# Narrow back transposes, 1/std spread by matmuls, and earlier loads at three stage borders of a ConvNeXt block with a fixed-point convolution behind it

## The chip, the cores and the metric

The kernel runs on one core of a Trainium2 chip. The metric is the device time of one execution in microseconds; the median of three runs of the kernel before is 1080.56 us (1080.2 to 1081.1).

## What is computed

```python
# x: (16, 96, 56, 56) fp32
y = depthwise_conv7x7(x, dw_w) + dw_b
y = transpose(y, (0, 2, 3, 1))                       # channels last
y = (y - mean_c(y)) * rsqrt(var_c(y) + 1e-6) * ln_w + ln_b
h = gelu(y @ w1 + b1)                                # 96 -> 384
gx = sqrt(sum over h,w of h*h)                       # per image and hidden channel
nx = gx / (mean_hidden(gx) + 1e-6)
h = grn_gamma * (h * nx) + grn_beta + h
z = x + transpose(h @ w2 + b2)
w = power_of_two(clamp(weight)); zq = floor(z * 65536) / 65536, clipped
out = depthwise_conv3x3(zq, w) + floor_to_fixed(bias)
```

## The kernel before, in words

Three stages run one after the other, with DRAM between them (`y_scratch`, `z_scratch`). All waits are semaphores written by hand; each engine runs its own instruction list in order.

**Stage a** is the 7x7 convolution. It goes over 24 batches of 4 channels (CB), and a batch has 4 groups s. `load_rows` (L321) brings 16 images of 4 channels into `xin`. `tin` (L552) turns them on TensorE, ACT's `xt_copy` (L691) and DVE's `low_part` (L894) split the result into a high and a low fp32r part. Each channel is then convolved by 12 matmuls (`convolve`, L573) with banded weight tables. The tables come from the 49 taps: DVE writes them into `la` (L832), SP stores `la` to DRAM as `lines_a` (L341 to L343) and reads it back shifted, one diagonal per partition (`load_tables`, L354); ACT rounds them (`table_high`, L722), POOL makes the remainder (`table_low`, L471). ACT evicts each channel with its bias (`yt_copy`, L706). `back` (L600) turns each group of the previous batch back with 8 transposes of 64 pixels x 112 rows, alternating between partitions 64 to 127 and 0 to 63; ACT's `out_copy` (L716) reads 56 of each 64 columns, reversed, into `ost`, and SP stores the batch (L371). In its loop SP loads batch b+1 and stores batch b-3. Beside this DVE and POOL keep a running mean and a running sum of squares over the 96 channels (`update`, L919, L921, L923, and POOL's L486), with pixels on the partitions and 448 columns: 28 pairs of rows of 16 images.

**Between a and the MLP** one chain makes 1/std for all 448 columns: variance on DVE (L929), square root on ACT (L765), reciprocal and a Newton step (L942 to L946), reordering (`in_order`, L938), 8 transposes (L634), a copy (L950), a store to DRAM (`stats_scratch`, L767) and loads that broadcast each image's row to 96 partitions (`rb`, L771 to L773). SP loads `y` of image 0 (L401) after all stores of y have landed.

**The MLP** goes over 16 images of 7 tiles of 448 pixels. `scale` (L964, y times 1/std), `high` (L969) and POOL's `low` (L497) feed `up` (L643 to L645, 9 matmuls of a tile), ACT applies gelu (L787) and sums squares (`squares`, L755). `step(i)` runs `up` of image i beside `down` (L653, 3 fp32 matmuls of a tile) of image i-1, because the global response norm needs the sums of a whole image: `grn_sums` (L977), POOL's square root (L506), a matmul with ones (L667), `grn_scale` (L983 to L994). Hence in `step(0)` TensorE has no `down` to run. DVE rounds and SP stores z (`store_z`, L417); ACT's `with_constant` (L762) scales x for the residual.

**Stage c** is the 3x3 convolution, built like a with 4 matmuls for a channel, its own tables (L523 on POOL) and evictions shared by ACT and DVE (L1079, L1068). It starts when the last z has landed: SP loads batch 0 of z, DVE clears the halos of `xt` (L812). SP loads the tables of batch b in turn b, and stores batch b-3.

## Time and profile before

| | |
|---|---|
| median of 3 runs | 1080.56 us |
| the profiled execution, its own time | 1080.37 us |
| span of the profile | 1078.6 us |
| TensorE busy | 990.8 us (92%) |
| VectorE, ScalarE busy | 825.5 us, 830.8 us (77% each) |
| GpSimd busy | 411.7 us (38%) |
| mean granted clock of TensorE | 0.963 |

The profile is one execution. Its page gives busy shares in 40 slices, and the trace behind it gives each instruction with its start, its length and what released it. Engines: PE is TensorE, PEld its weight loads, DVE VectorE, ACT ScalarE, POOL GpSimd, SP SyncE; a q behind the name means the queue that issues a DMA. "us from start" counts from the first instruction. A merged row "x8" begins with the first of eight instructions and lasts until the end of the last.

### The profile page before, as it was taken

The numbers are of one execution on the slowest core, as the hardware profiler recorded it, in microseconds if no ns is written. First come the engines' busy times: TensorE is split into PE (matmuls) and PEld (weight loads), VectorE is DVE, ScalarE is ACT, GpSimd is POOL, SyncE is SP. The second block draws the span as 40 slices with busy tenths as digits, with TensorE's granted clock in tenths as the row PEclk, the third lists the DMA queues.
The fourth block names the chain that finished last, engine by engine and source line by source line (L and its number), as shares of the span: only waits on it lengthen the run. The fifth ranks groups of instructions, "written<-read, shape, count | busy, mean of one in ns | idle before, by whom it ended". The sixth has DMA issues, their size and how long they took to land.

```text
span 1078.6 us, 21092 instructions
## 1 busy us (share of the span) xinstructions
PE 990.8 (92%) x5574; PEld 717.7 (67%) x5574; DVE 825.5 (77%) x1768; ACT 830.8 (77%) x1724; POOL 411.7 (38%) x353
## 2 busy tenths in 40 slices
PE   3999999999999467999999999999999849999996
PEld 2788888888888355666666666666666427767774
DVE  7777777777777565888888888888887667888885
ACT  2688888888887357898988888888888607787874
POOL 2666676666666153332333333333332001111110
PEclk9999999999999766999999999999999978999999
DMA  8777777777772592555555555555543247999995
GB/s 162 147 183 182 181 179 184 187 187 179 180 179 66 131 225 82 157 175 163 172 162 171 172 162 170 162 171 162 167 136 90 80 110 187 245 248 243 247 244 154
DMA packets 146312, 182.95 MB, mean 170 GB/s; under 512 B 13799, under 2 KB 140424, under 8 KB 143208
## 3 DMA queue, kind: packets, MB, share of 16 engines
q1 hardware_dynamic: 145480, 179.97, 62.5%
q10 hardware_dynamic: 800, 2.61, 1.0%
q8 instruction: 13, 0.21, 0.1%
q14 instruction: 19, 0.16, 0.0%
HBM read 124.28 MB, written 58.25 MB: 169 GB/s over the span
## 4 chain that ended last, share of the span: by engine, by line
PE 71%; DVE 12%; ACT 6%; issue 6%; DMA 3%; DVEq 1%; POOL 0%; ACTq 0%; SPq 0%; POOLq 0%
PE psum L573 22%; PE psum L653 21%; PE psum L643 6%; PE psum L644 6%; PE psum L645 6%; PE psum L552 6%; PE psum L600 3%; DVE arena_r L894 3%; ACT arena L706 2%; ACT arena_r L691 2%; DVE arena L919 1%; DMA arena<-lines_a 1%; DVE arena L923 1%; DVE arena L1079 1%; DVE arena L1068 1%
## 5 line engine op out<-in xcount | busy, mean ns | idle before, releaser
L573 PE MATMUL psum<-arena_r 112*128 112x464 f32 x1536 | 375.2, 386 | 0.3 <-issue 0.2
L573 PEld LDWEIGHTS psum<-arena_r 112*128 112x128 f32 x1536 | 276.8, 190 | 33.9 <-issue 1.1
L653 PE MATMUL psum<-arena,w2s 128*96 128x448 f32 x672 | 266.8, 542 | 2.8 <-DVE w2s L994 2.8
L787 ACT ACTIVATE arena<-psum,b1g 128x448 f32<-128x448 f32 x336 | 201.8, 630 | 58.3 <-PE psum L645 58.2
L497 POOL TENSOR_TENSOR arena_r<-arena,arena_r 96x448 fp32r<-96x448 f32 x112 | 134.1, 1197 | 268.7 <-DVE arena_r L969 194.8
L653 PEld LDWEIGHTS psum<-arena,w2s 128*96 128x96 f32 x672 | 109.8, 164 | 119.1 <-issue 111.8
L643 PE MATMUL psum<-arena_r,w1h 96*128 96x448 f32 x336 | 154.1, 459 | 14.2 <-POOL arena_r L497 13.0
L706 ACT ACTIVATE arena<-psum,bias_a 64x224 f32<-64x224 f32 (+1 forms) x288 | 117.0, 442 | 61.8 <-PE psum L573 50.6
L894 DVE TENSOR_TENSOR arena_r<-psum,arena_r 112x224 fp32r<-112x224 f32 x384 | 127.2, 382 | 48.3 <-ACT arena_r L691 47.5
L691 ACT ACTIVATE arena_r<-psum 112x224 fp32r<-112x224 f32 x384 | 112.6, 355 | 54.8 <-PE psum L552 52.5
L486 POOL TENSOR_TENSOR arena<-arena 128x448 f32<-128x448 f32 x96 | 110.0, 1146 | 109.8 <-DVE arena L923 109.2
L552 PE MATMUL psum<-ident,arena 112*112 112x112 f32 x768 | 109.1, 278 | 43.1 <-DMA arena<-in_x_dram 16.0
L755 ACT ACTIVATE arena<-arena 128x1792 bf16<-128x1792 f32 (+1 forms) x96 | 144.5, 1505 | 2.2
L471 POOL TENSOR_TENSOR arena_r<-arena,arena_r 112x512 fp32r<-112x512 f32 x96 | 123.6, 1300 | 20.5 <-ACT arena_r L722 20.5
L644 PE MATMUL psum<-arena_r,w1h 96*128 96x448 f32 x336 | 126.2, 376 | 0.0
L645 PE MATMUL psum<-arena_r,w1l 96*128 96x448 f32 x336 | 125.9, 375 | 0.0
L552 PEld LDWEIGHTS psum<-ident,arena 112*112 112x112 f32 x768 | 77.9, 139 | 58.0 <-issue 21.9
L919 DVE TENSOR_TENSOR arena<-arena,psum 128x448 f32<-128x448 f32 x96 | 59.6, 621 | 74.3 <-ACT arena L706 74.2
L706 ACT ACTIVATE arena<-psum,bias_c 64x224 f32<-64x224 f32 (+1 forms) x216 | 88.0, 442 | 15.8 <-PE psum L573 13.9
L1002 DVE TENSOR_TENSOR psum<-arena,psum 96x448 f32<-96x448 f32 x112 | 69.6, 621 | 39.5 <-PE psum L653 39.0
L600 PEld LDWEIGHTS psum<-ident,arena 64*112 64x112 f32 x1536 | 57.5, 130 | 62.7 <-issue 57.8
L523 POOL CAST arena_r<-arena 112x1024 fp32r<-112x1024 bf16 x24 | 25.0, 1043 | 180.3 <-DMA arena<-lines_c 153.7
(94 smaller groups left out, 1146.1 us busy)
## 6 DMA issues: line engine op xcount, KB each, us to landing
arena<-lines_a SPq DMA_DIRECT2D x48, 448.0 KB
arena<-in_x_dram SPq DMA_DIRECT2D x48, 392.0 KB
y_scratch<-arena SPq DMA_DIRECT2D x48, 392.0 KB
arena<-in_x_dram SPq DMA_DIRECT2D x112, 168.0 KB, 2.5
z_scratch<-arena SPq DMA_DIRECT2D x112, 168.0 KB, 2.0
arena<-z_scratch SPq DMA_DIRECT2D x48, 392.0 KB
out_dram<-arena SPq DMA_DIRECT2D x48, 392.0 KB
arena_r<-y_scratch SPq DMA_DIRECT2D x98, 168.0 KB, 2.6
```

Source lines behind the costliest of these rows:

```text
L497: pool.tensor_tensor(yl[:, CH * t:CH * t + CH], ct[:, (t + p) % 2, :], yh[:, CH * t:CH * t + CH].bitcast(F32), ALU.subtract).then_inc(yn_r ...
L552: mm = nc.tensor.transpose(p_in[s % 2][0:PAIR, at:at + CM], xin[:, p, IG // 2 * s + i, PAIR * h:PAIR * h + PAIR], ident[0:CM, 0:CM])
L573: mm = nc.tensor.matmul(p_conv[s % 2][:, 0:NCOL], w[:, p, s, TW * k:TW * k + TW], v[:, p, s, slot0 + k:slot0 + k + JP, :].rearrange("p j i ...
L643: nc.tensor.matmul(p_h[m][:, 0:CH], w1h[:, w], yh[:, cols], start=True, stop=False)
L644: nc.tensor.matmul(p_h[m][:, 0:CH], w1h[:, w], yl[:, cols], start=False, stop=False)
L645: nc.tensor.matmul(p_h[m][:, 0:CH], w1l[:, w], yh[:, cols], start=False, stop=True).then_inc(h_done, 1)
L653: mm = nc.tensor.matmul(p_o[k][0:C, 0:CH], w2s[:, p, m, :], hid[:, p, m, CH * t:CH * t + CH], start=(m == 0), stop=(m == MT - 1))
L691: ins = nc.scalar.activation(tile_group(xt_h, p, s, h), bank_group(s, h), ACT.Identity)
L706: ins = nc.scalar.activation(to[part, q], cols[part, :, :, j:j + 2 * NRUN - 1:2], ACT.Identity, bias=bias[part, bass.ds(n, 1)], scale=scale)
L755: nc.scalar.activation(sqd[:, 0:CH * (t1 - t0)], hid[:, p, m, CH * t0:CH * t1], ACT.Square, accum_out=ss[:, p, m, part:part + 1]).then_inc ...
L787: nc.scalar.activation(hid[:, p, m, CH * t:CH * t + CH], p_h[m][:, 0:CH], ACT.Gelu, bias=b1g[:, m:m + 1]).then_inc(gelu_done, 1)
L894: ins = dve.tensor_tensor(tile_group(xt_l, p, s, h), bank_group(s, h), tile_group(xt_h, p, s, h).bitcast(F32), ALU.subtract)
```

## The change

It has eight parts.

1. **Back transposes** (stages a and c) take 56 pixels, not 64; the tables are read with another offset so that the 56 results lie at columns 0 to 55. `forwards` follows.
2. **Start.** The eleven small loads go from SP's queue to ACT's; ACT issues them first, and waits for them only before its first `yt_copy`. DVE clears the halos, then writes `la` with one strided copy in place of 49. The first four tables are loaded each by its own pair of DMAs (`t_first`). `convolve` waits for each channel's table alone. ACT runs one square root at the start.
3. **Stores** run at b-2 in place of b-3, in both stages; in c the tables are loaded one batch ahead.
4. **Last batch of a.** Its four backs use two pairs of PSUM banks in turn. The last update leaves out the mean.
5. **The chain for 1/std** runs first for the 56 columns of images 0 and 1 (EARLY), between ACT's `out_copy` of groups 0 and 1 of the last batch; the other 392 follow in pieces between DVE's tiles of image 0 (`other_images`).
6. **Spread.** For images 0 and 1, 1/std reaches the 96 partitions through TensorE: for each tile 8 fp32 matmuls, with one column of `rstd` broadcast as a weight of 56 x 96 and the reversed identity `rev` (56 x 56) as the moving side. `scale` reads the result in PSUM. Two tiles come before `up(0, 0)`, one behind each `up(0, t)`, five behind `step(0)`. The rows for the other images are turned (4 transposes), copied and stored to DRAM after image 1's `scale` and `high`; ACT waits for that store before the gelu of image 1.
7. **y of image 0** goes to a place of its own (`y0`): channels 0 to 87 from DRAM once 22 batches are stored, the last 8 channels straight from `ost`, in 8 DMAs of one channel each. SP's order around it is new.
8. **Border to c.** z of images 0 to 13 and the first tables are loaded before the last image's `down`; POOL clears the halos; TensorE doesn't wait for the last residual; only images 14 and 15 (one pair of columns) are loaded after the last store of z.

```diff
@@ offsets and narrow back
-    return bass.AP(tensor=v.tensor, offset=v.offset + LSTEP - 1,
-                   ap=[part, [LSTEP, n], [bank, 2], [-1, W]])
+    return bass.AP(tensor=v.tensor, offset=v.offset + W - 1,
+                   ap=[part, [W, n], [bank, 2], [-1, W]])
...
-                            mm = nc.tensor.transpose(outs[s % len(outs)][0:CM, 1 - r, LSTEP * n:LSTEP * n + LSTEP],
-                                                     yt[q:q + LSTEP, p, i, (h + 1 - r) % 2].rearrange("p g m -> p (g m)"),
-                                                     ident[q:q + LSTEP, q:q + LSTEP])
+                            mm = nc.tensor.transpose(outs[s % len(outs)][0:CM, 1 - r, W * n:W * n + W],
+                                                     yt[q:q + W, p, i, (h + 1 - r) % 2].rearrange("p g m -> p (g m)"),
+                                                     ident[q:q + W, q:q + W])
@@ SP, start and stage a
+            for k in range(CB):
+                for r in range(2):
+                    shifted = bass.AP(tensor=lines_a, offset=k * (KA * TW) + LPAD + r * LSTEP - (W - 1), ap=[[1, W], [1, KA * TW]])
+                    sp.dma_start(toep[W * r:W * r + W, 0, k, :], shifted).then_inc(t_first[k], 16)
...
-                        if not (isinstance(b, int) and b < 3):
-                            store(b - 3, 1 - s)
+                            tables(b + 1, 1 - s)
+                        if not (isinstance(b, int) and b < 2):
+                            store(b - 2, s)
...
+            def first_y(b):
+
+                sp.wait_ge(stages["a"]["out"], G * b + 1)
+                for k in range(CB):
+                    c = CB * b + k
+                    sp.dma_start(y0[c:c + 1, :].rearrange("o (m t) -> o m t", t=RUN),
+                                 ost[CR // CB * k:CR // CB * (k + 1), b % 2, 0, :]).then_inc(y0_in, 16)
+
+            sp.wait_ge(stages["a"]["st0"], 32 * (LATE // 2 + LATE % 2))
+            sp.wait_ge(stages["a"]["st1"], 32 * (LATE // 2))
+            sp.dma_start(y0[0:CB * LATE, :], y_v[0][0:CB * LATE]).then_inc(y0_in, 16)
+            for b in range(LATE, NBATCH):
+                first_y(b)
+                store_y(b, b % 2)
...
-            load_y(0, 0)
-            sp.wait_ge(r_in[0], 16)
-            load_y(1, 1)
+            sp.dma_start(yraw[:, 1, :], y_v[1]).then_inc(y1_in, 16)
             for t in range(NCH):
                 load_x(0, t)
+            sp.wait_ge(stat_rows, 1)
+            sp.dma_start(st_dram.ap().rearrange("(g i) (m t) -> (i m) g t", i=IG, t=PAIR),
+                         res1.rearrange("p (g t) -> p g t", g=G)).then_inc(stat_out, 16)
+            sp.wait_ge(stat_out, 16)
@@ SP, border to c
+            sp.wait_ge(o_done, NCH * (NIMG - 1))
+            for k in range(4):
+                sp.wait_ge(z_out[k], 16 * Z_USES[k % 2] * (NIMG // 2 - 1))
+            first_rows(0, NI2 - 1, c_early)
+            tables_c(0, 0)
             step(NIMG, 0, more_y=False, more_x=False)
             for k in range(4):
                 sp.wait_ge(z_out[k], 16 * Z_USES[k % 2] * NIMG // 2)
-            load_rows(stages["c"], z_v, 0, 0)
-            sp.wait_ge(halo, 2)
+            first_rows(NI2 - 1, NI2, stages["c"]["x0"])
@@ TensorE
+            def spread(i, t):
+
+                n = NCH * i + t
+                to = p_spread[n % 2]
+                if n == 1:
+                    pe.wait_ge(stages["a"]["out"], C)
+                need(pe, scale_done, n - 1)
+                for k in range(4):
+                    m, h = 2 * t + k // 2, k % 2
+                    for half in range(2):
+                        at = 2 * NRUN * ((h + half) % 2) + NRUN * i + m
+                        rows = slice(LSTEP * half, LSTEP * half + W)
+                        mm = nc.tensor.matmul(to[:, half, W * k:W * k + W], rstd[rows, at:at + 1].to_broadcast([W, C]), rev[rows, :],
+                                              start=True, stop=True)
+                mm.then_inc(spread_done, 1)
...
                     if t < NCH and not tail:
                         up(i, p, t)
+                    if head and t < NCH:
+                        spread(*divmod(t + 2, NCH))
...
+                if head:
+                    for t in range(2, NCH):
+                        spread(1, t)
+                    stat_rows_out()
@@ ScalarE
+            act.wait_ge(prep, 3)
+            nc.scalar.activation(gnx[:, :], halves[:, :], ACT.Sqrt)
...
-                        out_copy(NBATCH - 1, s, 1)
+                        if s == 1:
+                            act.wait_ge(var_ready, 1)
+                            nc.scalar.activation(root[:, 0:EARLY], var[:, 0:EARLY], ACT.Sqrt).then_inc(root_ready, 1)
+                        out_copy(NBATCH - 1, s, 1, p_last)
...
                 need(act, o_done, NCH * (i - 1))
+                if fixed and i == 1:
+                    act.wait_ge(stat_out, 16)
@@ VectorE
-            for dy in range(7):
-                for dx in range(7):
-                    at = (dy + 1) * LSTEP + dx - 3
-                    ins = dve.tensor_copy(la[:, at:at + 1], wa[:, 7 * dy + dx:7 * dy + dx + 1])
-            link(ins)
...
                 if head:
                     for t in range(1, NCH):
                         normalise(0, 0, t)
+                        other_images(t - 1)
                     for t in range(NCH):
-                        if t == NCH - 1:
-                            grn_sums(i, p)
                         normalise(1, 1, t)
+                    statistics_out()
+                    grn_sums(i, p)
                     return
```

## Rows read from the trace of the kernel before

**Rows 1.** The page, part 2: busy tenths and granted clock in 40 slices.
```profile
PE   3999999999999467999999999999999849999996
PEclk9999999999999766999999999999999978999999
```

**Rows 2.** Sums by stretch: us, busy (x) by engine, clock, DMA share, GB/s.
```profile
30.00:330.00 300.00, 296.91 (x2043) 243.29 (x2042) 224.98 (x436) 240.95 (x595) 205.03 (x171) 0.99 0.71 177
900.00:1078.00 178.00, 162.48 (x1478) 120.29 (x1476) 140.60 (x341) 134.09 (x380) 22.94 (x22) 0.99 0.86 229
```

**Rows 3.** Timeline of the start: us from start, length, engine, line, [idle before].
```profile
5.51 3.05 DVE L832 COPY arena<-arena 96x1 f32<-96x1 f32 x49
...
11.25 0.76 SPq L354 DMA_DIRECT2D arena<-lines_a  x2
...
23.67 3.76 PE L573 MATMUL psum<-arena_r 112*128 112x464 f32 x12
...
26.59 0.63 ACT L722 ACTIVATE arena_r<-arena 112x512 fp32r<-112x512 f32 x1 [2.92 <-DMA arena<-lines_a]
```

**Rows 4.** Timeline of TensorE, end of stage a; the last row is a later back.
```profile
346.05 0.44 PE L600 MATMUL psum<-ident,arena 64*112 64x64 f32 x8
346.42 2.79 PE L573 MATMUL psum<-arena_r 112*128 112x464 f32 x12
...
363.67 0.64 PE L600 MATMUL psum<-ident,arena 64*112 64x64 f32 x8 [0.64 <-ACT arena L716]
```

**Rows 5.** Timeline in stage c: TensorE waiting once in a batch.
```profile
1057.14 0.59 PE L552 MATMUL psum<-ident,arena 112*112 112x112 f32 x4 [0.35 <-DVE arena_r L894]
```

**Rows 6.** Timeline between stage a and the first up.
```profile
359.77 0.62 DVE L919 TENSOR_TENSOR arena<-arena,psum 128x448 f32<-128x448 f32 x1 [1.15 <-ACT arena L706]
...
374.66 0.40 ACTq L767 DMA_DIRECT2D stats_scratch<-arena  x1
...
379.21 0.34 ACTq L771 DMA_DIRECT2D arena_r<-stats_scratch  x1
...
382.92 0.62 DVE L964 TENSOR_TENSOR arena<-arena_r 96x448 f32<-96x448 f32 x1 [8.29 <-DMA arena_r<-stats_scratch]
...
385.29 0.74 PE L643 MATMUL psum<-arena_r,w1h 96*128 96x448 f32 x1 [11.32 <-POOL arena_r L497]
```

**Rows 7.** Sums by stretch, columns as in rows 2: the last stored batch.
```profile
349.00:353.00 4.00, 4.00 (x32) 3.15 (x31) 2.26 (x4) 2.44 (x6) 1.63 (x2) 1.00 0.72 192
353.00:357.00 4.00, 4.00 (x26) 3.30 (x25) 2.21 (x4) 2.65 (x7) 1.84 (x2) 1.00 0.00 0
```

**Rows 8.** Timeline: small matmuls with weight loads (96 columns, fp32).
```profile
36.95 0.59 PE L539 MATMUL psum<-bet,w2r 128*96 128x1 f32 x6
```

**Rows 9.** Timeline of the head of the MLP.
```profile
391.46 0.61 DVE L964 TENSOR_TENSOR arena<-arena_r 96x448 f32<-96x448 f32 x1
...
393.25 0.61 DVE L964 TENSOR_TENSOR arena<-arena_r 96x448 f32<-96x448 f32 x1
...
414.34 0.59 PE L667 MATMUL psum<-gx,ones 128*128 128x3 f32 x2 [4.92 <-POOL gx L506]
...
421.65 2.48 PE L653 MATMUL psum<-arena,w2s 128*96 128x448 f32 x6
```

**Rows 10.** Sums by stretch, columns as in rows 2: the granted clock in the head.
```profile
390.00:394.50 4.50, 4.50 (x13) 3.98 (x13) 4.40 (x6) 1.95 (x4) 3.85 (x3) 0.50 0.99 231
394.50:400.00 5.50, 5.50 (x28) 4.98 (x28) 5.13 (x7) 5.43 (x9) 3.86 (x4) 1.00 1.02 257
416.00:421.80 5.80, 5.80 (x17) 5.05 (x17) 2.08 (x6) 3.65 (x6) 1.45 (x1) 0.50 0.00 0
```

**Rows 11.** Timeline of the border to stage c.
```profile
878.87 1.84 SPq L321 DMA_DIRECT2D arena<-z_scratch  x4
...
885.29 1.72 PE L552 MATMUL psum<-ident,arena 112*112 112x112 f32 x8 [12.70 <-DMA arena<-z_scratch]
...
891.63 1.90 PE L573 MATMUL psum<-arena_r 112*128 112x464 f32 x4
```

More of the change, by code:

```diff
@@ L198, in build @@
         sqd = mlp(128, SQ_WIDE // 2).bitcast(BF16)
+        hid = [hid0, mlp(128, MT, HW)]
+        y0 = hid[1][0:C, MT - 1, :]
+        ct = mlp(C, 2, CH)
+        rstd, var, root, rstd_in, newton, res1 = [conv(TW, NPIX) for _ in range(6)]
+        res1 = res1[0:IG * NPAIR, :]
+        assert conv.at <= mlp.at - 2 * CH - HW
         BANK = 512
@@ L215, in build @@
         dw_in = sem("dw_in")
+        t_first = [sem(f"t_first{k}") for k in range(CB)]
         consts = sem("consts")
@@ L362, in tables_c, with conv_transfers @@
                 load_tables(stages["c"], lines_c, KC, toep_b, b, s)
-            def conv_transfers(S, src, dst, tables, ahead):
+            def conv_transfers(S, src, dst, tables):
                 runs_of = dst.rearrange("(i g) c (m t) -> g (c m) i t", g=2, t=RUN)
@@ L485, in add @@
                     need(pool, m2_done, n)
-                    pool.tensor_tensor(m2, m2, dsq[:, k % 2, :], ALU.add).then_inc(m2_done, 1)
+                    cols = slice(EARLY, NPIX) if last and k == 2 * CB - 1 else slice(0, NPIX)
+                    pool.tensor_tensor(m2[:, cols], m2[:, cols], dsq[:, k % 2, cols], ALU.add).then_inc(m2_done, 1)
             bodies(pool, add)
@@ L512, in _ @@
             steps(pool, step)
+            pool.wait_ge(h_done, MT * NCH * NIMG)
+            for v in (xt_h, xt_l):
+                for slots in (slice(0, HALO), slice(HALO + NPAIR, SLOTS)):
+                    pool.memset(v[:, :, :, slots, :].bitcast(F32), 0.0).then_inc(halo, 1)
             S = stages["c"]
@@ L545, in tin @@
                     n = G * b + s
-                    if s == 0:
+                    if S is stages["c"] and isinstance(b, int) and b == 0:
+                        if s == 0:
+                            pe.wait_ge(c_early, 32)
+                        if s == G - 1:
+                            pe.wait_ge(S["x0"], 32)
+                    elif s == 0:
                         pe.wait_ge(S[f"x{p}"], 16 * (b - p) + 32)
@@ L636, in _ @@
-            mm.then_inc(stat_t, 1)
+                    if S is stages["c"]:
+                        back_waits(NBATCH - 1, s)
+                        back(NBATCH - 1, s, 1)
+                    else:
+                        if s == 0:
+                            evicted(pe, S, NBATCH - 1, CB - 1)
+                        pe.wait_ge(S["out"], G * (NBATCH - 1) + max(s - 1, 0))
+                        back(NBATCH - 1, s, 1, p_last)
+            conv_stage(stages["a"], KA, 0, ((toep_h, xt_h), (toep_h, xt_l), (toep_l, xt_h)), bias_products)
@@ L950, in _, with other_images @@
-            dve.tensor_copy(res1.rearrange("p (g h w) -> p g h w", g=G, h=2), forwards(p_stat[0:IG * NPAIR], G)).then_inc(stat_rows, 1)
+            inverse(early)
+            refine_square(early)
+            refine(early).then_inc(first_ready, 1)
+            dve.wait_ge(m2_done, C)
+            dve.tensor_scalar(var[:, EARLY:NPIX], m2[:, EARLY:NPIX], 1.0 / C, LN_EPS, ALU.mult, ALU.add).then_inc(var_ready, 1)
+            def other_images(k):
+                middle = (EARLY + NPIX) // 2
+                if k == 0:
+                    dve.wait_ge(root_ready, 2)
+                    inverse(slice(EARLY, middle))
+                elif k == 1:
+                    inverse(slice(middle, NPIX))
+                elif k == 2:
+                    refine_square(slice(EARLY, NPIX))
+                elif k == 3:
+                    link(refine(slice(EARLY, NPIX)))
+                elif k == 4:
+                    in_order(rstd_in, rstd).then_inc(stat_in, 1)
```

217 lines of the change are left out of this document (115 added, 102 removed).

## The prediction

> **What bounds the kernel now.** I read the page's slices first, then sums by stretch, then the timeline at each border. The slices [rows 1] show TensorE at nine tenths nearly everywhere, with three holes: the first slice, the fourteenth and fifteenth (stage a to MLP) and the thirty-third and its neighbours (MLP to stage c). The granted clock falls only at the last two. Inside stage a TensorE is busy 296.91 of 300 us, inside stage c 162.48 of 178 with the DMA rate at 229 GB/s [rows 2]. So two kinds of time can be won: TensorE's own work in a and c, and the length of the holes. In steady MLP nothing is changed. The sum is made against the profiled execution, 1080.37 us (span 1078.6, 1.8 around it), which is 0.2 below the median of 1080.56; I don't correct for that.
>
> **Start.** DVE spends 3.05 us on 49 one-column copies; the tables' first loads are issued at 11.25; the first convolution starts at 23.67; ACT then waits until 26.59 for the tables of batch 1 and sits ahead of the eviction that TensorE needs [rows 3]. The order of the bytes is the point: x of batch 0, small loads, `la`, tables 0, x 1, tables 1. `la` is ready some 5 us earlier (3.05 for the copies, the rest because halo, mean and m2 memsets now stand elsewhere), but its store lies behind the 0.8 MB of x in SP's queue, and the small loads, now on ACT's queue, share the DMA engines with that x. What goes away is the idle time between the end of those loads and the tables, about 1.5 to 2.5 us. Bounds: 0.8 (all hidden behind x) and 3.05 (the whole copy row). Eight table loads in place of two cost six more issues (0.38 each, half of the 0.76 row), in which x 1 is issued later, but the queue is full then. I take **2.0**.
>
> **Narrow back.** Eight transposes last 0.44 and the next convolution starts 0.37 after them; at half clock the eight last 0.64 [rows 4]. The extra 0.20 for one halving of the clock, over four pairs (the two halves of the partitions run side by side), is about 0.05 a pair, that is 64 columns at two clocks each at 2.4 GHz (53 ns). With 56 columns a pair takes 47 ns: 4 x 6.7 = 27 ns less for a group. In stage a TensorE never waits, so 96 groups give **2.6**. Ends: 0 if the weight load sets the pace (its 112 columns stay), 0.37 x 8/64 = 46 ns x 96 = 4.4 if the whole row shrinks. The granted clock fits the moving side, so I stay at 27 ns.
>
> The Trainium skill, "TensorE: Matmul & The Clock Gate", section "LDWEIGHTS (loading the stationary operand)", says that a weight load takes time by its columns, and that the rows don't matter. By it, 112 columns at 1.2 GHz would be 93 ns a load, as before the change, and the narrow back would bring nothing. The pair step of about 53 ns [rows 4] lies below that figure, so the trace speaks against it as the bound here; it is a rival below because only the load's width is unchanged.
>
> In stage c TensorE waits 0.35 us in a batch for DVE's `low_part` [rows 5]. Two of the four backs of a batch lie on the stretch between DVE's release and that wait, so what they save is waited for; the other two count: 2 x 27 ns x 24 = 1.3, up to 2.6 with all four, 0 if DMA binds (229 GB/s). I take 1.6. Stores one batch earlier and tables one batch ahead move SP's issues: SP now stops about one channel for `out`, but its next load is a batch away, so 0. Stage c: **1.6**.
>
> **Border a to MLP.** Before, DVE's last `dev` starts at 359.77, the stats store is issued at 374.66 and lands at 379.21 (4.55), the broadcasts let the first `scale` start at 382.92, and the first `up` starts 2.37 later, at 385.29 [rows 6]. After:
> - The early chain has 56 columns and leaves out the mean, a table load and the transposes. I estimate 363; it is not what comes last.
> - y0: batch 21's store is over by 353, as the DMA is empty from 353 to 357 at a rate of 192 before [rows 7]. 88 channels are 1.10 MB, at 192 GB/s 5.7 us plus some 2, so 361. Batch 22's store (0.8 MB, 4.2 us) stands ahead of the last four one-channel loads in the same queue: 360.3 + 1 + 4.2 + a little = 366.3. This comes last. First `scale` 366.3 (16.6 earlier), first `up` 368.7.
> - Then TensorE has more work: 14 spreads of 8 fp32 matmuls, 16 instructions each with its load. Six small ones with 96 weight columns take 0.59 [rows 8]; less about 0.2 for the last one's own length, over five steps, that is some 80 ns apart. 16 x 80 = 1.3 alone; if the halves overlap, half of it, 0.65; 1.6 with a turn at each end. I take 1.3, and 2.4 at half clock. At 1.2 GHz an `up` takes 9 x 0.373 = 3.36, at 2.4 GHz 1.86: 13 matmuls in 4.50 and 28 in 5.50 [rows 10]. The clock returned at 394.5, 9.2 after the first `up`. So two tiles at half clock, 2 x (3.36 + 2.4) = 11.5, and five at 1.86 + 1.3 = 15.8, with 0.5 for ACT's squares: the last of nine spreads ends at about 396.5.
> - Image 1's tiles follow at the pace of DVE and POOL, 1.79 (391.46 to 393.25) [rows 9], five after the first: its last `scale` is over at 406, `high` 406.6, the copy 407.2 (0.6, a DVE copy of 448 columns as the tile row), the store of the rows 4.55 on [rows 6]: 411.8.
> - A new wait: ACT may not start the gelu of image 1 before that. Queued behind it on ACT are `with_constant` and all gelus, and TensorE's `up(1, 1)` waits for the banks. So 411.8 + 1.3 = 413.1, then two `up` at half clock, 6.7, or 5.0 at ACT's pace: the first `down` at 418.1 to 419.8. Before it was 421.65 [rows 9]. SP waits for the same store with `load_next(2)` and `store_z` behind it; DVE needs image 2 only with the first `down`, 3 us later, so 0.
> Of 16.6 us won at the head's start only **3.0** are left. The `grn_sums` chain (414.34 before) is ready by about 409 and no longer decides.
>
> **Border to c.** Before, z of batch 0 and 1 (1.6 MB) is issued at 878.87, the first turn of x starts at 885.29, the first convolution at 891.63, since `tin` of batch 1 stands ahead of it [rows 11]. After, 0.70 MB of that is there already and POOL clears the halos (DVE's part was hidden behind z's landing). 0.70 MB at 170 to 190 GB/s is 3.7 to 4.1. Of this some 0.8 goes back: more matmuls of the first batch run before the clock returns. **3.2**, between 1.5 and 5.5. The extra issues on SP (4, 1.8 us) fall between the last load of x and the first store of image 15, where SP waits for DVE anyway. If that were full, the store would be late by as much, but z's ring has four slots.
>
> **Sum.** 2.0 + 2.6 + 3.0 + 3.2 + 1.6 = 12.4. 1080.37 - 12.4 = **1068.0**.
>
> **Rivals.**
> - *A quick head*: halves of the spreads overlap (0.65) and the clock is back two tiles earlier. Nine spreads then end about 5 us earlier and the two `up` run at full clock. The border gives 9: 1062.0. For it: pairs overlap in the back [rows 4]. Chance 0.2.
> - *A slow head*: spreads 1.6, clock up a tile later, DVE's tiles longer with the pieces of `other_images` between (5.6 us in all). 4 us back: the border gives -1 to 0, the start 1: 1072.5. Chance 0.2.
> - *The weight load sets the back's pace*: no 2.6, no 1.6: 1072.2. Chance 0.05.
> - *Slower*: the spreads are small matmuls between loads; if the clock stays at 1.2 GHz through the whole head, seven tiles take 7 x (3.36 + 2.7) = 42.4 from 368.7, five spreads 13.5 more, to 424.6, then 7.6 for turning, copy, store and ACT, and 6.7 for two `up`: the first `down` at 438.9, 17.3 later than before. With 9.4 won elsewhere the time is 1088.3. It decides as soon as the head loses more than 9.4. Against it: continuous `up` brought the clock back before [rows 10]. Chance 0.03. That 56 rows would break the overlap of the two halves (0.16 for a group, 31 us over both stages) belongs to the same side: 0.02.
> - *The change doesn't do what it says*: y0 lands late, as some wait on SP stands ahead; then the head starts later, up to 3 us: 1071. It counts with the slow head.
> The forecast itself has 0.5.
>
> **How the numbers follow.** Range 1060.5 to 1075: from a quick head with 1.5 more at the start and in c, down to a slow head with both c terms at their low end. About 0.8 of the chance lies in it. A measurement can tell some 0.2% (2 us) from no change. Faster 0.93, same 0.02, slower 0.05.
>
> **What would show it.** Back rows of 0.41 in place of 0.44 and a period of a channel at the end of a of 3.06 in place of 3.09; tables' first loads issued near 9.7; the first `scale` near 366.3 behind a y load; spreads of about 1.3 at 2.4 GHz; ACT's wait ahead of image 1's gelu on the stats store; first `down` near 418.7; first convolution of c about 4 us after the last store of z less than before. It is wrong if y0 isn't the last to come, if the clock is at 1.2 GHz during image 0 for more than 12 us, or if the period of stage a doesn't shrink.

## The result: 58 us slower

The changed kernel takes 1138.55 us (median of 4 runs, 1138.03 to 1140.16) against 1080.58: a ratio of 1.0539, interval 1.052 to 1.0557. The forecast was 1068.0. The profiled execution has a span of 1138.3 against 1078.6, so 59.7 us have to be found.

The page's slices, as in [rows 1], with the DMA row of both kernels (the last line is the DMA row of the kernel before). A slice is 28.5 us here, 27.0 before:

```profile
PE   2999999999998999999999999999997768768766
PEclk9999999999998559999999999999999798987888
DMA  7377677777764325555555555555324676675674
...
DMA  8777777777772592555555555555543247999995
```

The hole between stage a and the MLP (14th and 15th slice before) is nearly filled, but the clock there is lower. From the 31st slice on, TensorE is at six to eight tenths where stage c had it at nine. DMA is not full there either, at four to seven tenths where it was at nine. The sums by stretch, as in [rows 2], say the same: stage a is as before, and in stage c TensorE is busy 139.17 of 178 us in place of 162.48, at 172 GB/s in place of 229.

```profile
30.00:330.00 300.00, 296.11 (x2044) 243.61 (x2044) 221.07 (x434) 241.37 (x595) 204.98 (x171) 0.99 0.69 173
900.00:1078.00 178.00, 139.17 (x1122) 104.63 (x1123) 108.79 (x264) 106.21 (x301) 18.06 (x18) 0.88 0.67 172
```

From the start times of TensorE's matmuls in both traces (first and last convolution of a stage, first and last `down`) the 59.7 us split as follows (changes in us, less is faster):

| stretch | before | after | forecast | measured |
|---|---|---|---|---|
| start, to the first convolution | 23.67 | 24.80 | -2.0 | +1.1 |
| stage a, first to last convolution | 334.43 | 333.96 | -2.6 | -0.5 |
| last convolution of a to first `down` | 63.55 | 67.65 | -3.0 | +4.1 |
| first to last `down` | 450.40 | 450.26 | 0 | -0.1 |
| last `down` to first convolution of c | 19.58 | 15.78 | -3.2 | -3.8 |
| stage c, first to last convolution | 175.80 | 234.58 | -1.6 | +58.8 |
| last convolution to the end | 11.17 | 11.27 | 0 | +0.1 |

Each column is one trace. Other kernels below run the same code in some of these stretches, and their traces show the spread: with the changed start the first convolution comes at 23.8 to 25.1, the changed stage a takes 334.0 to 334.9, and the stretch up to the first `down` 66.2 to 67.7. The kernel before and before_c_store2, alike up to stage c, differ there by 0.3, 0.6 and 1.2. A difference under about 1 us between two traces is therefore not shown.

**Stage c.** The timeline of SP's queue and of TensorE's `tin` (us from start, length, engine, line, [idle before <- what ended it]). The changed kernel: SP's rows, then the `tin` with which TensorE begins three successive batches.

```profile
948.87 0.90 SPq L366 DMA_DIRECT2D out_dram<-arena  x2
950.05 3.36 SPq L329 DMA_DIRECT2D arena<-z_scratch  x2
953.61 0.98 SPq L349 DMA_DIRECT2D arena<-lines_c  x2
956.33 0.90 SPq L366 DMA_DIRECT2D out_dram<-arena  x2
957.78 3.18 SPq L329 DMA_DIRECT2D arena<-z_scratch  x2
961.16 0.93 SPq L349 DMA_DIRECT2D arena<-lines_c  x2
969.44 0.90 SPq L366 DMA_DIRECT2D out_dram<-arena  x2
970.62 3.34 SPq L329 DMA_DIRECT2D arena<-z_scratch  x2
...
958.97 1.74 PE L585 MATMUL psum<-ident,arena 112*112 112x112 f32 x8 [4.54 <-DMA arena<-z_scratch]
...
967.46 0.98 PE L585 MATMUL psum<-ident,arena 112*112 112x112 f32 x8
...
979.52 1.74 PE L585 MATMUL psum<-ident,arena 112*112 112x112 f32 x8 [4.54 <-DMA arena<-z_scratch]
```

Every load of z (L329) is issued 1.2 to 1.5 us behind a store (L366), never on its own. Two batches take 979.52 - 958.97 = 20.55 us, 10.3 for one in place of 7.46 before. The loop can be read off: `tin` 958.97, then 10.5 us until the output is ready and the store goes out at 969.44, the load behind it at 970.62, and 8.9 us until that load lets the next `tin` start. The sum of what SP waited for (900 to 1100 in the changed kernel; us in total, times, longest):

```profile
SPq L366 <- DVE arena L1181: 89.2, 19, 10.0
SPq L329 <- PE psum L585: 0.5, 1, 0.5
```

The same of before, 900 to 1078:

```profile
SPq L371 <- DVE arena L1068: 45.4, 24, 6.5
SPq L321 <- PE psum L552: 39.1, 20, 4.6
```

Before, SP arrived early at the load and waited there for TensorE to leave the buffer (39.1 us in 20 waits). Now it waits only at the store: it always comes too late to the load.

In stage a (60 to 340) the waits moved in the same way, first the changed kernel, then before:

```profile
SPq L366 <- ACT arena L796: 157.8, 20, 8.3
SPq L329 <- PE psum L585: 3.5, 2, 2.0
...
SPq L321 <- PE psum L552: 93.1, 19, 5.3
```

There the later loads cost nothing: a batch of stage a lasts 13.9 us, and TensorE waits for x only 0.4 us in all.

### The profile page after: what moved, and what is told of

Its sections match the earlier page's. It is cut to its first block, busy times and chain, and to the rows that moved or that the text cites. A ratio compares the mean times of both kernels' runs of the same rounds, so it can differ in the third digit from the quotient of the medians.

```text
span 1138.3 us, 21578 instructions
## 1 busy us (share of the span) xinstructions
PE 1033.3 (91%) x5794; PEld 755.6 (66%) x5794; DVE 816.8 (72%) x1715; ACT 832.6 (73%) x1725; POOL 410.0 (36%) x360
## 4 chain that ended last, share of the span: by engine, by line
PE 68%; DMA 10%; DVE 9%; ACT 5%; issue 4%; SPq 3%; DVEq 0%; ACTq 0%; POOL 0%; POOLq 0%
PE psum L710 20%; PE psum L606 20%; DMA arena<-z_scratch 7%; PE psum L700 7%; PE psum L701 6%; PE psum L702 6%; PE psum L585 5%; ACT arena L786 3%; PE psum L633 2%; DMA arena<-in_x_dram 2%; SPq L329 2%; DVE arena_r L967 2%; PE psum L683 1%; DVE arena L1181 1%; DVE arena L998 1%
## 5 line engine op out<-in xcount | busy, mean ns | idle before, releaser
L606 PE MATMUL psum<-arena_r 112*128 112x464 f32 x1536 | 384.4, 393 | 0.3 <-issue 0.2
L606 PEld LDWEIGHTS psum<-arena_r 112*128 112x128 f32 x1536 | 283.6, 195 | 32.3 <-issue 1.0
L520 POOL TENSOR_TENSOR arena_r<-arena,arena_r 96x448 fp32r<-96x448 f32 x112 | 131.1, 1170 | 279.3 <-DVE arena_r L1085 202.4
L585 PE MATMUL psum<-ident,arena 112*112 112x112 f32 x768 | 117.0, 292 | 83.7 <-DMA arena<-z_scratch 51.8
L700 PE MATMUL psum<-arena_r,w1h 96*128 96x448 f32 x336 | 157.6, 469 | 4.9 <-POOL arena_r L520 3.2
L585 PEld LDWEIGHTS psum<-ident,arena 112*112 112x112 f32 x768 | 84.0, 147 | 97.5 <-issue 57.1
L493 POOL TENSOR_TENSOR arena_r<-arena,arena_r 112x512 fp32r<-112x512 f32 x96 | 123.7, 1301 | 20.4 <-ACT arena_r L804 20.4
L701 PE MATMUL psum<-arena_r,w1h 96*128 96x448 f32 x336 | 129.0, 384 | 0.0
L702 PE MATMUL psum<-arena_r,w1l 96*128 96x448 f32 x336 | 128.6, 383 | 0.0
L633 PEld LDWEIGHTS psum<-ident,arena 56*112 56x112 f32 x1536 | 58.8, 135 | 66.0 <-issue 61.9
```

The lines of the kernel that those rows point to most:

```text
L493: pool.tensor_tensor(toep_l[:, p, s, :], toep[:, p, s, :], toep_h[:, p, s, :].bitcast(F32), ALU.subtract).then_inc(A["tl"], 1)
L520: pool.tensor_tensor(yl[:, CH * t:CH * t + CH], ct[:, (t + p) % 2, :], yh[:, CH * t:CH * t + CH].bitcast(F32), ALU.subtract).then_inc(yn_r ...
L585: mm = nc.tensor.transpose(p_in[s % 2][0:PAIR, at:at + CM], xin[:, p, IG // 2 * s + i, PAIR * h:PAIR * h + PAIR], ident[0:CM, 0:CM])
L606: mm = nc.tensor.matmul(p_conv[s % 2][:, 0:NCOL], w[:, p, s, TW * k:TW * k + TW], v[:, p, s, slot0 + k:slot0 + k + JP, :].rearrange("p j i ...
L700: nc.tensor.matmul(p_h[m][:, 0:CH], w1h[:, w], yh[:, cols], start=True, stop=False)
L701: nc.tensor.matmul(p_h[m][:, 0:CH], w1h[:, w], yl[:, cols], start=False, stop=False)
```

## Experiments on the slow stage c

**c_store3**, the changed kernel with stores of c at b-3:

```diff
-                        if not (isinstance(b, int) and b < 2):
-                            store(b - 2, s)
+                        if not (isinstance(b, int) and b < lag):
+                            store(b - lag, (s + lag) % 2)
```

`lag` is 3 in stage c and 2 in stage a.

> Edit: the changed kernel, but in stage c batch b-3 is stored in body b, as before the change, where the changed kernel stores batch b-2 (tables stay one batch ahead, stage a stays as changed). Theory (the store of b-2 waits for an output that TensorE finishes only a batch later, and the load behind it on SP's queue starts too late): stage c falls back to its old length, 187 us from its first convolution at about 892.5, so 1080 to 1082 us, ratio to the changed kernel 0.949 to 0.951; SP's wait at the store no longer stands just ahead of each load, and TensorE's wait for the z load (44.8 us) goes. Rival (tables moved one batch ahead, or the narrow back, lengthen stage c): stays near 1138.

Measured: 1079.6 us, ratio to before 0.9997 (0.9987 to 1.0007). Stage c takes 175.10 us. SP waits at the load again:

```profile
SPq L366 <- DVE arena L1181: 50.8, 24, 6.6
SPq L329 <- PE psum L585: 40.3, 20, 5.0
```

The one line is worth 59 us, and the rest of the change is worth nothing in sum.

**c_tables_behind**, tables of c in turn b again, stores left at b-2:

```diff
-                            tables(b + 1, 1 - s)
+                            if ahead:
+                                tables(b + 1, 1 - s)
+                        if not ahead and not (isinstance(b, int) and b == 0):
+                            tables(b, s)
```

> Edit: the changed kernel, but in stage c the tables of batch b are loaded in body b, as before the change; the stores stay at b-2. Theory (store order): nothing is won, 1135 to 1141 us. Rival (two table loads between x and the store make the queue late): near 1081 us.

Measured: 1160.72 us (one run). Both were wrong: it is 22 us slower still. The tables of the batch now stand behind the late load too. So the tables one batch ahead, which I had no price for, soften the loss.

**before_c_store2**, the kernel before with only c's stores moved to b-2:

```diff
-                        if not (isinstance(b, int) and b < 3):
-                            store(b - 3, 1 - s)
+                        if not (isinstance(b, int) and b < lag):
+                            store(b - lag, (s + lag) % 2)
```

`lag` is 2 in stage c and 3 in stage a.

> Edit: the kernel before the change, with one thing changed: in stage c batch b-2 is stored in body b. Theory (store order alone makes the loss): stage c takes 10.2 to 10.3 us for a batch in place of 7.46, so 1080.6 + 22 x 2.8 = 1136 to 1142 us. Rival (the loss needs the tables ahead or the narrow back as well): below 1100 us.

Measured: 1159.78 us (one run), 79 more than before and 18 above the theory's range. The store order alone makes the loss; the theory had taken its size from the changed kernel, whose tables are ahead. c_tables_behind, 0.9 away, is the same case.

**c_pool_store**, the same lag of two, but stores of c issued by POOL, behind its copy of the tables:

```diff
+                    if not (isinstance(b, int) and b < 2):
+                        store(b - 2, p)
...
+            def store(b, s):
+                pool.wait_ge(S["out"], G * b + G)
+                for g in range(2):
+                    pool.dma_start(out_of[g][bass.ds(b * CR, CR)], ost[CR * g:CR * g + CR, s, :, :]).then_inc(S[f"st{s}"], 16)
```

> Edit: the changed kernel (stores of batch b-2 in body b), but in stage c the stores are issued by POOL, behind its copy of the tables of batch b, so that no load stands behind them. Theory (only the order on SP's queue makes the loss: a load waits behind a store whose output isn't ready): 1078 to 1084 us. Rival (storing b-2 rather than b-3 is bad in itself, since store and load then fall together on the DMA engines): 1130 us or more.

Measured: 1081.91 us (one run). Bytes, buffers and lag are those of the changed kernel; only the load no longer stands behind the store and its wait for `out`. In c_store3 the stores do stand ahead of the loads on SP's queue, but of a batch that is ready sooner, and nothing is lost. The two together settle it: it is a load behind a wait on one queue, not the traffic. DMA is back at 241 GB/s between 900 and 1050 (c_store3: 240, the changed kernel: 175).

## Experiments on the other terms

**before_narrow**, the kernel before with the narrow back alone (the first part of the change, with the copy of the turned statistics adapted).

> Edit: the kernel before the change, with the narrow back alone (56 columns a transpose in place of 64, both stages). Theory of the prediction (moving columns set the pace): 2.6 us less in stage a and 1.6 in c, 1076.4 us, ratio 0.9961. Rival (the weight load, whose 112 columns stay, sets the pace): 0 to 0.8 us less, 1079.8 to 1080.6; the period of a batch in stage a of the changed kernel, 13.88 against 13.90, speaks for this one.

Measured: 1079.21 us, ratio 0.9994 (0.9985 to 1.0003). Stage a takes 334.07 us in place of 334.43, stage c 175.08 in place of 175.80. A back is 0.42 or 0.43 us in place of 0.44 [rows 4]:

```profile
345.26 0.42 PE L600 MATMUL psum<-ident,arena 56*112 56x56 f32 x8
345.61 2.80 PE L573 MATMUL psum<-arena_r 112*128 112x464 f32 x12
348.34 0.43 PE L600 MATMUL psum<-ident,arena 56*112 56x56 f32 x8
```

The rival of the weight load is nearer in its number. An eighth of the moving columns is gone, and the stages are 0.36 and 0.72 us shorter where 2.6 and 1.6 were forecast; the first of these is within the spread of one trace. The start times of the transposes are firmer: from the first of a group of eight to the last it is 216 ns before and 206 to 208 with the narrow back, so 8 to 10 ns of the 27 forecast for a group, or 0.7 to 0.9 us for the 96 groups of a stage (an estimate from these times). At 2.4 GHz two successive pairs start 56 ns apart with 64 columns and 54 to 55 with 56. At 1.2 GHz they start 107 ns apart with 64 columns (before) and 93 to 95 with 56 (the changed kernel): there the step did shrink by an eighth.

**c_border_late**, c_store3 with `first_rows` and the tables loaded only behind the last store of z (two blocks of SP's list exchanged).

> Edit: c_store3 without the early load at the border to c: the rows of batch 0 of images 0 to 13 and the tables are loaded only behind the last store of z, as before the change. Theory (the early 0.70 MB give the 3.8 us by which stage c starts sooner): the first convolution of c comes 3.5 to 4.2 us later than in c_store3, 1083 to 1084 us. Rival (POOL's clearing of the halos in place of DVE's gives it): no difference, 1079.6 us.

Measured: 1082.83 us, 3.2 more than c_store3; from the last `down` to c's first convolution 19.03 us in place of 15.50. The early load gives the border's gain, as forecast.

**head_warm**, c_store3 with TensorE kept busy before the first `up`:

```diff
+            def warm(times):
+                for _ in range(times):
+                    nc.tensor.matmul(bank[2][:, 0:HID], w1h[:, 0:128], w1h[:, :], start=True, stop=True)
...
                         back(NBATCH - 1, s, 1, p_last)
+                        warm((9, 1, 5, 3)[s])
...
+            warm(26)
             steps(pe, step)
```

> Edit: c_store3 with TensorE kept busy in the pauses between stage a and the first up: 44 matmuls of 384 columns whose results nobody reads (9, 1, 5 and 3 behind the four last backs of stage a, 26 behind the second spread). Theory (the pauses between 359.5 and 370.9 bring the clock to 0.5, and the spreads between the ups keep it there till 426): the granted clock stays at 1.0, a tile of image 0 takes 1.86 + 0.8 = 2.7 us in place of 5.12, then DVE, POOL and the stats store set the pace; first down at 404 to 410 in place of 426.4, so 1079.6 less 16 to 22: 1058 to 1064 us. Rival (spreads of 56 columns lower the clock by themselves): the clock falls to 0.5 some tiles in, less than 8 us won, above 1071 us.

Measured: 1072.04 us, ratio to before 0.9917 (0.99 to 0.9935). A gain of 7.6 us over c_store3, where the theory had 16 to 22; the number is the rival's, its mechanism is not, since the spreads between the `up` ran at 1.00. The granted clock fell all the same before them, behind the pause of 1.6 us that lies ahead of the first of these matmuls. At 1.2 GHz they took too long: the first `up` came at 378.21 in place of 370.61. By then the clock was up again, and a tile of image 0 took 2.82 us. At the end of the head ACT still waited 4.56 us for the store of the statistics' rows.

**head_light**, each spread replaced by two wide matmuls; it leaves out 1/std of images 0 and 1, so only its time is of use:

```diff
-                for k in range(4):
...
-                        mm = nc.tensor.matmul(to[:, half, W * k:W * k + W], rstd[rows, at:at + 1].to_broadcast([W, C]), rev[rows, :],
-                                              start=True, stop=True)
+                for half in range(2):
+                    mm = nc.tensor.matmul(to[:, half, :], w1h[:, 0:C], w1h[:, 0:4 * W], start=True, stop=True)
```

> Edit: c_store3 with each spread's eight fp32 matmuls of 56 columns replaced by two single-pass matmuls of 224 columns that write other numbers (1/std of images 0 and 1 is left out). Nothing keeps the clock up in the pauses. Theory (the many small matmuls between the ups keep the clock down): the clock is back at 1.0 some 9 us after the first up, near 379, as in the kernel before; first down near 402 to 408; 1056 to 1062 us. Rival (the clock stays at 0.5 for another reason, such as the head's waits): only the spreads' own length goes, 14 x 1.1 = 15.4 us at most, of which DVE's pace of 1.8 us a tile takes back some; the clock stays at 0.5 till past 400, and the first down comes at 412 or later: 1065 us or more.

Measured: 1067.1 us (one run). The time and the first `down` (412.49) lie in the rival's range, the clock does not: it came back at about 385, 15 us behind the first `up` and not 9, and fell again ten microseconds later (columns as in [rows 2], the granted clock third from the end):

```profile
384.00:390.00 6.00, 5.46 (x27) 4.78 (x26) 4.20 (x9) 5.24 (x9) 2.03 (x3) 0.91 0.00 0
390.00:396.00 6.00, 3.63 (x20) 2.66 (x18) 4.02 (x8) 6.00 (x10) 3.30 (x4) 0.95 0.00 0
396.00:402.00 6.00, 5.22 (x17) 4.36 (x17) 5.76 (x9) 4.27 (x7) 4.08 (x5) 0.50 0.00 0
```

From 390 to 396 ACT is busy all the time and TensorE 3.63 of 6 us; the clock is low behind that. So the many small matmuls do hold the clock down (with them it is 0.50 until about 417 in c_store3), but even without them it is slow to return, and once it is up, ACT's pace opens pauses and the clock is lost again.

**head_stat**, c_store3 with the statistics' rows turned and copied in the middle of image 1 and not at the end of the head:

```diff
+                    if head and t == NCH - 1:
+                        stat_rows_out()
```

> Edit: c_store3 with the turning of the statistics' rows right behind the spread of image 1's tile 1 on TensorE, and their copy on DVE behind tile 1 of image 1, in place of the end of the head on both. Theory (ACT's gelu of image 1 stands behind the stats store, and this sets the first down): the store is issued at about 408 in place of 415, ACT's wait of 6 us goes, and the first down comes 3 to 5 us sooner than 424.6: 1074.6 to 1076.6. Rival (at the low clock the spreads and ups themselves are the bound, and the wait hides behind them): less than 1 us.

Measured: 1078.74 us, ratio 0.9987 (0.9978 to 0.9997); last convolution of a to first `down` 65.4 us in place of 66.3. The rival: ACT's wait of 6 us is gone and 0.9 us are won, so at the low clock spreads and `up` are the bound and the wait lay mostly beside them.

**start_order**, c_store3 with the convolution of batch 0 ahead of the `tin` of batch 1, in both stages.

> Edit: c_store3 with one change of TensorE's order: in batch 0 of both stages the convolution of a channel stands ahead of the tins of batch 1. Theory (both stages' first convolution waits for x of batch 1, whose tin stands ahead of it, and not for the tables): stage a's first convolution starts near 21 in place of 24.1 (POOL is done with the low tables at 20.3), stage c's near 887 to 889 in place of 892.1; but the matmuls of batch 0 then run until the same x, so 1.5 to 4 us less in all: 1075.5 to 1078. Rival (the tables or the turned x of batch 0 are late too): both first convolutions move by less than 1 us.

Measured: 1079.35 us (one run). The first convolutions moved as the theory said, and stage a's further (16.62 in place of 24.07; 887.07 in place of 891.79), but stage a's last one starts at 358.71 in place of 358.30, and from the last `down` to c's last convolution it is 190.7 us in place of 190.6. An earlier first matmul is worth nothing while the second batch waits for the same load.

**start_x1**, c_store3 with x of batch 1 issued ahead of the tables.

> Edit: c_store3 with x of batch 1 issued in stage a right behind the store of the lines (near 4) and ahead of the tables' first loads, not behind them (13.9). Theory (x of batch 1 is what the start waits for): its landing moves from 22.6 to 15 or 16; the tables land 4 us later than now, at about 20; first convolution at 20 to 22 in place of 24.1; 2 to 4 us less, 1075.6 to 1077.6. Rival (the DMA queue is full until 22 whatever the order, so the tables take the place of x): first convolution at 24 or later, 1079 to 1081.

Measured: 1081.82 us. The first convolution starts at 19.07, better than expected, and the time is 2.2 us worse than c_store3's; stage a's last convolution starts at 361.47 in place of 358.30. What is late next is DVE. Its timeline and POOL's in start_x1:

```profile
17.57 0.16 DVE L922 TENSOR_TENSOR arena<-arena 96x9 f32<-96x9 f32 x1
17.76 1.28 DVE L924 TENSOR_TENSOR arena<-arena 96x9 f32<-96x9 f32 x1
...
21.54 1.20 DVE L928 TENSOR_SCALAR arena<-arena 96x9 uint32<-96x9 uint32 x1
22.77 0.17 DVE L929 TENSOR_TENSOR arena<-arena 96x9 f32<-96x9 f32 x1
...
27.87 1.27 DVE L969 TENSOR_TENSOR arena_r<-psum,arena_r 112x224 fp32r<-112x224 f32 x4
...
17.75 4.96 POOL L495 TENSOR_TENSOR arena_r<-arena,arena_r 112x512 fp32r<-112x512 f32 x4 [15.26 <-ACT arena_r L806]
23.45 2.56 POOL L495 TENSOR_TENSOR arena_r<-arena,arena_r 112x512 fp32r<-112x512 f32 x2 [0.73 <-ACT arena_r L806]
```

The setup of the bias and of c's weights on DVE stands ahead of the low parts of batch 1 and ends only at 27.9. Moving it was not tried.

**all_1**, c_store3 with start_order, start_x1, head_stat, and 36 of the matmuls of head_warm, the first eight of them right behind the last convolution:

```diff
+                        warm((8, 0, 2, 5)[s])
                         if s == 0:
                             evicted(pe, S, NBATCH - 1, CB - 1)
...
+            warm(3)
...
+            warm(18, bank[2])
             steps(pe, step)
```

> Edit: c_store3 with start_order, start_x1 and head_stat together, and with 36 matmuls of 384 columns whose results nobody reads in TensorE's pauses between 359.5 and 370 (8, 2 and 5 ahead of three of the last backs, 3 ahead of the first spread, 18 behind the second), so that the first of them run before the pause that lowered the clock in head_warm. Theory: head near full clock throughout, first up at 370 to 371 in place of head_warm's 378.2, a tile of image 0 2.82 us, first down 404 to 409 in place of 424.6 (15 to 20 less); start 2 to 5 less; border to c 2 to 4 less: 1051 to 1060 us. Rival (the clock falls anyway once the stage a matmuls end, so that the extra matmuls only delay the first up): head wins under 8, 1065 us or more.

Measured: 1058.31 us, ratio 0.9793 (0.9779 to 0.9806). From the last convolution of a to the first `down` 47.0 us, against 66.3 in c_store3 and 63.55 before. The granted clock is 1.00 until 399.

**cold**, all_1 without these 36 matmuls.

> Edit: all_1 without the 36 matmuls in the pauses before the first up; everything else as in all_1. Theory (the clock, kept up by these matmuls, gives the head's 20 us; head_stat alone gave about 1): the clock falls to 0.5 behind the end of stage a and stays there until about 420, a tile of image 0 takes 5.12 us again, the first down comes at 422 to 425 and the time is 1076 to 1079 us. Rival (the three changes of order give it together, since each alone only showed the next wait): below 1066 us.

Measured: 1076.02 us, ratio 0.9963 (0.995 to 0.9976). 17.7 us of all_1's gain hang on matmuls that compute nothing. They do so with head_stat in place: head_warm, without it, won 7.6. The three changes of order give 3.6 us together (c_store3 less cold), where one by one they gave 0.3, -2.2 and 0.9; why they give more together was not taken apart. The sums by stretch (us, busy by PE, PEld, DVE, ACT, POOL, then the granted clock, DMA share, GB/s), first all_1:

```profile
360.00:364.00 4.00, 3.93 (x51) 2.88 (x47) 3.23 (x9) 2.41 (x6) 1.05 (x1) 1.00 0.79 209
364.00:368.00 4.00, 4.00 (x45) 3.94 (x43) 0.74 (x2) 1.60 (x2) 0.00 (x0) 1.00 0.34 94
368.00:376.00 8.00, 6.93 (x57) 5.68 (x57) 5.94 (x8) 3.66 (x6) 3.41 (x3) 1.00 0.74 188
384.00:392.00 8.00, 7.88 (x96) 6.68 (x94) 4.51 (x11) 7.91 (x13) 3.41 (x3) 1.00 0.01 4
```

and cold:

```profile
360.00:364.00 4.00, 1.91 (x28) 1.64 (x28) 2.74 (x9) 2.65 (x7) 1.04 (x1) 0.69 0.82 218
364.00:368.00 4.00, 1.95 (x25) 1.77 (x23) 1.24 (x3) 1.13 (x1) 0.08 (x1) 0.50 0.38 94
368.00:376.00 8.00, 6.90 (x30) 5.79 (x31) 4.12 (x6) 2.16 (x4) 2.66 (x3) 0.50 0.74 191
384.00:392.00 8.00, 8.00 (x40) 6.68 (x39) 4.89 (x8) 2.53 (x4) 2.32 (x2) 0.50 0.01 2
```

The busy shares of 384 to 392 are alike (7.88 and 8.00 of 8), the work done is not: 96 matmuls against 40. A full busy row says nothing of the clock, which stands third from the end.

**warm_c**, all_1 without start_x1, and with 20, 15 and 8 such matmuls behind the `tin` of groups 1, 2 and 3 of c's batch 0.

> Edit: all_1 without start_x1, and with matmuls whose results nobody reads at the border to c as well: 20, 15 and 8 behind the tins of x of batch 0 (groups 1, 2 and 3). Theory: the granted clock stays at 1.0 from 860 to 876 where all_1 had 0.50 to 0.74; the first four channels of c take 1.3 us each in place of 1.9, 1 to 3 us less in c's first batch; the start is 1 to 2 us better or worse, within what start_x1 showed: 1055 to 1058 us. Rival (z of batch 1 landing near 870, not the clock, sets the start of c): c's last convolution moves by less than 0.5 us against its last down, 1058 to 1060 us.

Measured: 1060.07 us, ratio 0.9803 (0.9789 to 0.9816). The clock stays at 1.00 until 872, and yet from the last `down` to c's last convolution it takes 189.4 us in place of 190.1: 0.7 won, next to the rival's limit of 0.5. TensorE then waits for z of batch 1:

```profile
869.14 1.08 PE L611 MATMUL psum<-arena_r 112*128 112x464 f32 x4
872.13 1.25 PE L590 MATMUL psum<-ident,arena 112*112 112x112 f32 x8 [1.91 <-DMA arena<-z_scratch]
```

The rival's mechanism: there a load sets the start, and a faster engine only waits for it. The ratios of warm_c and all_1 overlap, so neither is shown to be the faster. The 1.8 us between their medians are no more than the difference that their traces show from stage a to the first `down` (48.8 and 47.0), where the two kernels do the same.

## Why the prediction was wrong

**Stage c (the step that failed).** "SP now stops about one channel for `out`, but its next load is a batch away, so 0." Neither half holds. One channel (1.9 us) is what SP waited for `out` before the change (45.4 us in 24 waits); now it is 4.7 on average and up to 10.0, part of it in a loop that is slow already. The half that costs the time is the second. The load of batch b+2 is wanted as soon as TensorE has turned batch b, which is in the middle of TensorE's batch b-1; before, SP stood ready and waited 2 us for it each time (39.1 us in 20 waits). The output of b-2 is complete only at the end of TensorE's batch b-1. A store of b-2 ahead of that load therefore holds it for the rest of the batch, and puts its 0.8 MB in front of it. I had counted the lead of SP in SP's turns and not in TensorE's, and so was off by one batch. A load issued there has one batch of TensorE to land in: 7.46 us in c, where it needs 8.9 and leaves 1.2 us behind the store. In stage a the same order makes the loads as late (SP waited 93.1 us at them before, 3.5 now), and it costs nothing, since a batch there lasts 13.9 us: stage a took 0.5 us less than before. I gave this no rival. The forecast's slower rivals were the clock and the pairs, and the price of a load that comes late was never worked out, although [rows 2] showed DMA at 229 GB/s in c: a stage where transfers take nearly all of the time has no room for one that starts late.

**Narrow back: 0.4 and 0.7 (before_narrow) in place of 2.6 and 1.6.** The term was mis-sized: 8 to 10 ns for a group in place of 27. In [rows 4] I had read the extra 0.20 us at half clock as moving columns, since a pair step of 53 ns is also what 64 columns at 2.4 GHz take. At 1.2 GHz that was right (107 ns, then 93 to 95). What failed is carrying it over to 2.4 GHz, where the step stays at 54 to 56 ns when the moving side shrinks. That the load of 112 columns sets it there fits, but no run changed the load's width. The Trainium skill ("TensorE: Matmul & The Clock Gate", section "LDWEIGHTS (loading the stationary operand)") says that a load takes time by its columns, which gives nothing for the narrow back; on the change's worth it was nearer than my reading. Its figure of 93 ns for 112 columns is not what a pair step takes here at 2.4 GHz (54 to 56 ns).

**Start: +1.1 in place of -2.0.** The loss itself is hardly clear of the spread (the changed start gives 23.8 to 25.1, the old one 23.2 to 23.7), but the gain is certainly missing. The tables were ready sooner (POOL ended with them at 20.4 in place of 23.6) and nobody waited for them. Before, tables and the turned x of batch 1 were ready together, at 23.6 and 23.8, so hastening one of them could win nothing. In both kernels `tin` of batch 1 stands ahead of the first convolution, and its x is issued behind the tables: at 12.04 before, at 13.90 now, since eight issues take 3.34 us. These issues I had called free because "the queue is full then". Both start_order and start_x1 move the first convolution by 5 us and more and win nothing, so what stands behind (x of batch 1, then DVE's setup) is the bound.

**Border a to MLP: +4.1 in place of -3.0.** The chain up to the first `up` went nearly as worked out: the first `scale` at 368.57 (366.3 forecast), released by the loads of y0, the first `up` at 370.93 (368.7). The wait of ACT for the stats store was there as well (6.04 us, until 418.29). What failed is "two tiles at half clock ... and five at 1.86 + 1.3". All seven ran at 1.2 GHz, 5.12 us each, and so did everything to 426. That is the slower rival's mechanism, to which I gave 0.03; its price was too high (first `down` at 426.41, not 438.9) because a spread between two `up` adds 1.8 us (5.12 less 3.36) and not 2.7, and in a row one takes 1.3. At 2.4 GHz it adds 1.0 (2.82 less 1.86), where I had 1.3. [rows 10] had shown the clock returning 9.2 us after the first `up`, with nothing but `up` to run; the change puts 16 small matmuls behind each. What the low clock costs is shown by all_1 and cold: 18 us.

**Border to c: -3.8 in place of -3.2.** Right, and c_border_late confirms the cause.

## What to carry to other kernels

A store that waits for a result must not stand ahead of a load on the same in-order queue unless the result is ready before the load's buffer comes free; count the lead in the batches of the engine that produces and frees, and if the queue never waits at the load, the loads are late. Whether that costs time depends on the length of a batch: a load needed 8.9 us in c, where a batch lasts 7.46; in stage a it lasts 13.9. Where TensorE has a pause ahead of dense work, read the granted clock and not the busy share: here 36 matmuls into PSUM banks that nobody read, starting before the pause, were worth 18 us. An earlier first instruction may be worth nothing until the next thing it meets has been found.

## What the hardware showed

- The clock. In the changed kernel TensorE has no idle time from 376 to 416, and the granted clock is 0.50 (1.2 GHz) all along:

```profile
376.00:416.00 40.00, 40.00 (x242) 34.02 (x241) 20.99 (x35) 20.69 (x30) 13.04 (x12) 0.50 0.18 45
```

With wide matmuls in place of the spreads (head_light, one run) it was back at about 385. Where the pauses before them are filled, the very same spreads run at 1.00 from 364 to 392 (all_1). So the spreads did not lower a clock that was up, they kept one down that was. The Trainium skill ("TensorE: Matmul & The Clock Gate", section "What's actually happening") says that activity releases the throttle; forty microseconds at a full busy share did not do it here.
- DVE and POOL. While POOL runs its `table_low` (17.75 to 22.7 in start_x1, four of 1.24 us), DVE's operations on 96 x 9 elements take 1.20 to 1.28 us in place of 0.17, tensor_tensor and tensor_scalar alike, as if each waited for the end of one of POOL's. The Trainium skill ("GPSIMD Engine Reference", section "Specifications") says that GpSimd shares its SBUF interfaces with VectorE, with contention for VectorE's instructions that have two SBUF inputs or run in a two-port mode. The rows agree for those with two inputs; whether the tensor_scalar ones run in such a mode no row shows. Even tiny operations took as long as a whole one of POOL's.
- With two buffers the late loads of this kernel have a rhythm of two batches: 7.5 us apart, then 13.1 (stores at 948.87, 956.33, 969.44), so TensorE's wait shows at every second batch only.
